# Statistics ahead of the previous norm, a third chunk finished before the last sum, and low halves on VectorE, at the ends of twelve stages

## The reference

```python
def _layernorm(x, axis=-1, eps=1e-05):
    m = jnp.mean(x, axis=axis, keepdims=True)
    v = jnp.var(x, axis=axis, keepdims=True)
    return (x - m) / jnp.sqrt(v + eps)
...
    x = x + 0.5 * _L2_ffn_ref(_layernorm(x, axis=-1), L2_ffn_Wr, L2_ffn_br, L2_ffn_W_up, L2_ffn_b_up, L2_ffn_W_down, L2_ffn_b_down)
    x = x + _L2_attn_ref(_layernorm(x, axis=-1), L2_attn_Wq, L2_attn_bq, L2_attn_Wk, L2_attn_bk, L2_attn_Wv, L2_attn_bv, L2_attn_Wo, L2_attn_bo)
    x = x + 0.5 * _L2_ffn_ref(_layernorm(x, axis=-1), L2_ffn_Wr, L2_ffn_br, L2_ffn_W_up, L2_ffn_b_up, L2_ffn_W_down, L2_ffn_b_down)
```

## Time and profile before

| | us |
|---|---|
| runs of the kernel before | 1792.59, 1788.51, 1789.74 |
| their median | 1789.74 |
| the profiled execution's own time | 1807.28 |
| its span, first to last instruction | 1805.5 |
| TensorE busy in the span | 1522.0 |
| VectorE busy | 1221.4 |
| ScalarE busy | 1022.6 |
| GpSimd busy | 625.2 |

### The profile page before, as it was taken

The page is one execution under the profiler, slowest core; times in us unless marked ns, Lnnn a source line. Parts: engine busy times, 40 slices in busy tenths (PEclk is TensorE's granted clock), DMA queues, the critical chain, the costliest instruction groups (busy, mean ns, idle before and its releaser), DMA issues. The chain is left out here.

```text
span 1805.5 us, 25127 instructions
## 1 busy us (share of the span) xinstructions
PE 1522.0 (84%) x8766; PEld 1050.0 (58%) x8766; DVE 1221.4 (68%) x2789; ACT 1022.6 (57%) x1826; POOL 625.2 (35%) x764
## 2 busy tenths in 40 slices
PE   4998699997899699849989966996696789996696
PEld 3776333333577588538869955995595322223596
DVE  5787688992788743473335956595686688883685
ACT  2653488885554455345537732773374388885274
POOL 3575311122487100123026724673424211111333
PEclk9999899998899799869989978997798899998698
DMA  3121534300220400010000000000564633300574
GB/s 112 46 74 31 118 42 53 53 1 3 84 75 30 158 1 1 0 47 1 1 1 12 1 1 1 2 1 1 154 193 124 158 62 53 53 1 1 135 204 149
DMA packets 100757, 101.05 MB, mean 56 GB/s; under 512 B 23344, under 2 KB 86360, under 8 KB 99769
## 3 DMA queue, kind: packets, MB, share of 16 engines
q1 hardware_dynamic: 97687, 93.39, 21.4%
q0 software_dynamic: 2944, 6.05, 0.9%
HBM read 87.60 MB, written 15.78 MB: 57 GB/s over the span
## 5 line engine op out<-in xcount | busy, mean ns | idle before, releaser
L2617 DVE TENSOR_REDUCE mx<-bank 128x1 f32<-128x512 f32 (+1 forms) x512 | 320.1, 680 | 56.6 <-PE bank L2408 55.8
L2554 ACT ACTIVATE e<-bank 128x512 f32<-128x512 f32 x512 | 273.1, 600 | 50.4 <-PE bank L2440 47.6
L2440 PE MATMUL bank<-qq,kk 99*128 99x512 bf16 (+1 forms) x512 | 164.2, 386 | 12.9 <-ACT e L2554 12.3
L1546 POOL TENSOR_TENSOR midl<-mid,midh 128x512 fp32r<-128x512 f32 (+1 forms) x96 | 126.1, 1320 | 78.4 <-ACT midh L1466 78.3
L2440 PEld LDWEIGHTS bank<-qq,kk 99*128 99x128 bf16 (+1 forms) x512 | 38.8, 97 | 161.9 <-ACT e L2554 123.1
L1051 DVE TENSOR_TENSOR hl<-q,hh 128x512 fp32r<-128x512 f32 x64 | 44.8, 701 | 125.6 <-ACT hh L1021 103.6
L95 PE MATMUL bank<-wdh,midh 128*128 128x256 f32 (+1 forms) x384 | 113.6, 296 | 9.7 <-DVE x L1530 9.7
L226 POOL TENSOR_SCALAR rs<-mv 128x4 f32<-128x4 f32 x48 | 11.4, 237 | 307.5 <-DVE mv L213 306.6
L97 PE MATMUL bank<-wdh,midl 128*128 128x256 f32 (+1 forms) x384 | 111.1, 289 | 0.0
L96 PE MATMUL bank<-wdl,midh 128*128 128x256 f32 (+1 forms) x384 | 110.9, 289 | 0.0
L2047 POOL DMA_INDIRECT token_y<-y,g x60 | 61.2, 1020 | 134.6 <-DVE y L2016 121.5
(11 more groups left out here) (406 smaller groups left out, 4514.0 us busy)
## 6 DMA issues: line engine op xcount, KB each, us to landing
w<-in_L_ffn_W SPq DMA_DIRECT2D x30, 512.0 KB
w<-in_L_ffn_W SPq DMA_DIRECT2D x30, 256.0 KB
qq<-scratch SPq DMA_DIRECT2D x18, 384.0 KB
w<-in_L_ffn_w_kernel SPq DMA_DIRECT2D x16, 344.0 KB
w<-in_L_ffn_w_kernel SPq DMA_DIRECT2D x16, 320.0 KB
wo<-in_L_ffn_wo_kernel SPq DMA_DIRECT2D x16, 320.0 KB
scratch<-e SPq DMA_DIRECT2D x34, 128.0 KB, 5.0
sorted<-in_unsorted SPq DMA_DIRECT2D x2, 1935.0 KB, 10.9
```

The lines of the kernel that those rows point to most:

```text
L1546: e.tensor_tensor(l[0:fn, o], mid[i % 2][0:fn, o], h[0:fn, o].bitcast(F32), ALU.subtract).then_inc(*l2_m_lo.tick(n, i, f))
L2440: e.matmul(b_bank(t, u, j), keys(kk[0:K], t, b)[:, k * 128:(k + 1) * 128], queries(qq[0:K], t, b), start=True, stop=True).then_inc(*at_b.t ...
L2554: e.activation(er[u][:, j * 512:(j + 1) * 512], b_bank(t, u, j), ACT.Exp, bias=0.0, scale=scale).then_inc(*at_e.tick(n, t, u, j))
L2617: e.tensor_reduce(mxa[t % 3][:, o:o + nkb], bank[place_a["a", t, u, j]].rearrange("p (k n) -> p k n", k=nkb), X, ALU.max).then_inc(*at_max ...
```

## The change

Five edits, all at the stage ends:

- `finish_dve` takes the statistics of chunk c ahead of the norm of chunk c - 1, and for c = 3 also ahead of `pre.dve`.
- Stages 1, 3, 5 and 10 are marked `settled`. There VectorE does the norm of chunk 2 before the stage's last sum (`settle_dve`), and the transposes, copy and high half of chunk 2 follow those of chunk 1 at once. In the attention these now stand ahead of the last heads' turn and output product on TensorE and ScalarE.
- The low halves move from GpSimd to VectorE (`halve_dve`), those of layer 1's weights also. In settled stages the first stands ahead of the last sum, two between the statistics and the norm of chunk 3, and one behind that. At m = 9 (stage 8) two stand between statistics and norm, and two behind it. At m = 0 and m = 8 all four stand behind the norm.
- ScalarE writes the high half ahead of the features' copy where it is taken from `xn` (layers 0 and 3), and the copy of `lg` comes last.
- At m = 10 TensorE's closing matmuls stand between the transposes of chunks 1 and 2, not behind those of chunk 3.

SyncE's queue is unchanged, and so are the numbers of operations in all but the engine that does the low halves.

```diff
@@ finish_pe, finish_act: a settled stage also does chunk 2 at its last sum @@
                     features_pe(q, m, c - 2, stage)
+                    if c == 3 and stage.settled:
+                        features_pe(q, m, 2, stage)
...
                     features_act(q, m, c - 2, stage)
                     pre.halve_act(q, c - 2)
+                    if c == 3 and stage.settled:
+                        features_act(q, m, 2, stage)
+                        pre.halve_act(q, 2)
+
+        def settle_dve(q, m, pre):
+
             if m < LAST:
+                norm_dve(q, m, 2)
+                pre.halve_dve(q, 0)
+
+        def finish_dve(q, m, c, pre, ready=None, settled=False):
+            if m < LAST:
+                q.wait_ge(*(ready or xsum.at(m, c)))
+                stats_dve(q, m, c)
                 if c == 3:
                     pre.dve(q)
-                if c > 0:
+                    if settled:
+                        pre.halve_dve(q, 1)
+                        pre.halve_dve(q, 2)
+                    elif scalar_norm(m, 2):
+                        pre.halve_dve(q, 0)
+                        pre.halve_dve(q, 1)
+                if c > 0 and not (c == 3 and settled):
                     norm_dve(q, m, c - 1)
-                q.wait_ge(*(ready or xsum.at(m, c)))
-                stats_dve(q, m, c)
...
@@ begin_pe @@
             for c in range(CHUNKS):
-                if c >= 2:
+                if c == 2:
+                    pre.closing_pe(q)
+                if c == 3 or c == 2 and not stage.settled:
                     features_pe(q, m, c, stage)
...
-            pre.closing_pe(q)
 
         def begin_act(q, m, stage, pre):
             norm_act(q, m, 3)
...
-            for c in (2, 3):
+            pre.closing_act(q)
+            for c in ((3,) if stage.settled else (2, 3)):
+                if pre.from_norm:
+                    pre.halve_act(q, c)
                 features_act(q, m, c, stage)
-            pre.halve_act(q, 2)
+                if not pre.from_norm:
+                    pre.halve_act(q, c)
             if pre.route is not None:
                 q.wait_ge(*route_mm.at(m))
                 q.e.copy(lg_sb[:, :], bank[stage.banks["logits"]][:, 0:128]).then_inc(*logits.tick(m))
-            pre.halve_act(q, 3)
-            pre.closing_act(q)
-
-        def begin_dve(q, m, pre):
+
+        def begin_dve(q, m, stage, pre):
             norm_dve(q, m, 3)
+            for c in range(3 if stage.settled else 2 if scalar_norm(m, 2) else 0, CHUNKS):
+                pre.halve_dve(q, c)
             pre.closing_dve(q)
-
-        def begin_pool(q, m, pre):
-            for c in (2, 3):
-                pre.halve_pool(q, c)
...
@@ layer 1's weights @@
-            def pool(q):
-                low(q, "w1", w_lo)
-                low(q, "w2", w_lo)
+            def closing_dve(q):
+                low(q, "w1", w_set)
+                low(q, "w2", w_set)
...
@@ attention, PE and ACT @@
+                finish_pe(q, m, 3, stage, nxt)
                 if kind == 0:
                     turn(3, bank[0])
                 put_out(3, bank[1], otr[1])
-                finish_pe(q, m, 3, stage, nxt)
...
+                finish_act(q, m, 3, stage, nxt)
                 if kind == 0:
                     turn(3, bank[0])
-                finish_act(q, m, 3, stage, nxt)
...
@@ attention, DVE @@
                     elif s == "o" and u == 3:
+                        if i == 15:
+                            settle_dve(q, m, nxt)
                         close(i)
```

More of the change, by code:

```diff
@@ L68, with __init__ @@
 class Stage:
-    def __init__(self, pe, act, dve, pool, sp, banks=None, free=None):
+    def __init__(self, pe, act, dve, pool, sp, banks=None, free=None, settled=False):
         self.pe, self.act, self.dve, self.pool, self.sp = pe, act, dve, pool, sp
-        self.banks, self.free = banks, free
+        self.banks, self.free, self.settled = banks, free, settled
 class Pre:
-    def __init__(self, sp, buf, pe=None, act=None, dve=None, pool=None, late=None, issue=None, route=None, early=None, halve_act=None, halve_pool=None, loaded=None,
+    def __init__(self, sp, buf, pe=None, act=None, dve=None, pool=None, late=None, issue=None, route=None, early=None, halve_act=None, halve_dve=None, from_norm=False, loaded=None,
                  closing_pe=None, closing_act=None, closing_dve=None):
@@ L83, in __init__ @@
         self.sp, self.buf, self.route, self.loaded = sp, buf, route, loaded
-        self.early, self.halve_act, self.halve_pool = (f or none for f in (early, halve_act, halve_pool))
+        self.from_norm = from_norm
+        self.early, self.halve_act, self.halve_dve = (f or none for f in (early, halve_act, halve_dve))
         self.pe, self.act, self.dve, self.pool, self.late, self.issue = (f or nothing for f in (pe, act, dve, pool, late, issue))
@@ L1070, in down @@
                 def down(c):
+                    if c == 3:
+                        settle_dve(q, m, nxt)
                     for j in range(4):
@@ L1111, in free @@
                     q.wait_ge(*xt_set.at(m, what - 2))
-            stage = Stage(pe, act, dve, pool, sp, {0: 6, 1: 7, 2: 6, 3: 7, "logits": 0}, free)
+            stage = Stage(pe, act, dve, pool, sp, {0: 6, 1: 7, 2: 6, 3: 7, "logits": 0}, free, settled=True)
             return stage, nxt
@@ L2662, in dve @@
                 add(3, bank[1])
-                finish_dve(q, m, 3, nxt)
+                finish_dve(q, m, 3, nxt, settled=True)
             def pool(q):
@@ L2807, in attention @@
             banks = {0: 7, 1: 2, 2: 7, 3: 2, "logits": 3}
-            stage = Stage(pe, act, dve, pool, sp, banks, free)
+            stage = Stage(pe, act, dve, pool, sp, banks, free, settled=True)
             return stage, nxt
@@ L2861, in dve_program @@
                 finish_dve(q, 0, c, first_pre, ready=x_in[c].at())
-            begin_dve(q, 0, first_pre)
+            begin_dve(q, 0, start, first_pre)
             barrier(q, 0)
@@ L2866, in dve_program @@
                 if n + 1 < LAST:
-                    begin_dve(q, n + 1, nxt)
+                    begin_dve(q, n + 1, s, nxt)
                     barrier(q, n + 1)
@@ L2872, in pool_program @@
                 finish_pool(q, 0, c, first_pre)
-            begin_pool(q, 0, first_pre)
             barrier(q, 0)
```

24 lines of the change are left out of this document (10 added, 14 removed).

## The result

| | before | with the change |
|---|---|---|
| median of the runs, us | 1791.16 (4 runs, 1788.51 to 1792.87) | 1763.95 (4 runs, 1762.92 to 1765.77) |
| ratio, 95% interval | | 0.9844, 0.9828 to 0.9860 |
| span of the profiled execution | 1805.5 | 1761.0 |
| granted clock, mean | 0.920 | 0.931 |

The kernel is 27.2 us faster, 1.5%. Two more comparisons, on chips where the kernel before took 1792.3 and 1808.9, gave 0.9839 (0.9815 to 0.9864) and 0.9841 (0.9816 to 0.9865). Forecast were 1765.8 and 24 us.

The account below looks back on a forecast made before the run. Inside stages TensorE was taken as nearest the bound, at the twelve ends unhidden chains before the barrier. Terms summed to 23.9 us, taken as 24 off 1789.7: 1765.8 us, likely 1761 to 1771, range 1754 to 1778 with rivals.

Parts of the forecast that it names:

- the likeliest case: Whole kernel: the shortened end chains come off the span in full, about 1761 to 1771 us; chance 0.59.
- Statistics: End of stage 1: chunk 3's statistics start right after the last sum, not behind chunk 2's norm; 0.93 us less.
- The stalled norm: End of stage 1: chunk 3's norm, no longer beside a GpSimd low half, takes 1.11 instead of 2.05; 0.94 less.
- The tail: End of stage 1: only the barrier is left behind the copy of `lg`; 1.95 less about 0.15, 1.8 us less.
- The blocked `rs`: End of stage 1: two low halves on VectorE hold back GpSimd's addition and power; 0.9 us more, between nothing and 1.4.
- ScalarE's order in the attention: Stage 1: ScalarE does chunk 1 and 2's copies and high halves before the last heads' copy; 0.1 more, at most 1.2.
- Opening: Opening: TensorE's pitch of 3.65 us a chunk decides instead of VectorE's 4.8; 5.1 of 30.83 us less.
- Stage 9: End of stage 9: taking the closing matmuls' results apart lies beside chunks 2 and 3's transposes; 1.2 less, 0.3 to 2.0.
- Stage 0: End of stage 0: norm's chain over 1 us shorter, but query and key pieces stored 1.25 later; 0.7 less, 0 to 1.5.
- A: Stage ends: shorter idle pieces let transposes and router run at 2.4 GHz; 12 us more gain, 1754; chance 0.17.
- B: Next stages' starts, waiting for transfers or the cold clock, give half the gain back; 12 us, 1777.8; chance 0.17.
- C: Stage openings stay longer at 1.2 GHz, making the kernel slower than before; 11 us slower, 1801; chance 0.04.

Follow-up runs that it names:

- second pair: The kernel before and the changed kernel, each unchanged and profiled a second time; 1790.45 us and 1762.51 us.
- first pair: First profiles of the kernel before and of the changed kernel; profiled spans 1805.5 and 1761.0 us.
- third of the change: Third profile of the changed kernel, unchanged, on another chip; 1779.26 us beside 1808.85 for the kernel before.
- five parts undone one at a time: The changed kernel with, in turn: norm ahead of statistics, 0.9881; no stage settled, 0.9865; ScalarE's old order, 0.9901; closing matmuls last, 0.9863; low halves on GpSimd, 1769.29 us.

## Why the prediction was right

The number held (1765.8 against 1764.0, the range 1754 to 1778), and so did the likeliest case: one chain at each end, nothing beside it, and each us taken off it a us off the kernel. The sum of the ends fell by 29.7 us (28.9 for the second pair) and the runs by 27.2, 29.8 and 29.6. So the forecast of 24 was about 5 us too small: 1.5 at stage 9, 0.8 at the opening, 0.5 at stage 0 and small amounts elsewhere in the first pair, where another 1.5 at stage 3 are chance. Step by step:

- **Statistics, 0.93 an end**: 0.04 behind the sum at every end. Right. Undone where the stage isn't settled, it costs 3.0, since at stage 7 TensorE hides it. What settling gives (5.3, or 3.65 net of the blocked `rs`) the prediction had not priced apart.
- **The stalled norm, 0.94**: 1.11 or 1.12 at every end. Right.
- **The tail, 1.95 less 0.15 for the drain**: 0.09 remain, 1.86 less. Right, 0.06 too careful, at six ends.
- **The blocked `rs`, 0.9**: 0.63, 0.34 in the addition and 0.29 in the power. The mechanism was right, its size 0.27 too large: the power began when 0.43 us were left of the second low half, and came out 0.29 longer. At stage 5 only the addition is longer, 0.57.
- **ScalarE's order in the attention, 0.1 to 1.2**: 0.25. In stage 1 the last heads' copy starts 0.97 us behind TensorE's transposes of their output instead of 0.72. The faster output product ahead of the last sum, 0.9 us in stage 1 (0.65 against the second profile), more than pays for it; the prediction didn't have it.
- **Opening, 24.9 to 25.15 for 25.7**: pitch right (TensorE's 3.5 a chunk). From the first statistics to the barrier it is 17.90 us in all three profiles of the change and 23.14 and 23.17 before, 5.25 less for 5.1. The rest is the landing of the input (first statistics at 7.66 and 7.15 before, 6.96 to 7.25 with the change).
- **Stage 9, 1.2 with ends of 0.3 and 2.0**: 2.7, 1.7 and 2.4, above the upper bound in two of three profiles. This term was the worst sized. The bound counted the idle time behind the last closing matmul (1.45) and the copy, and not that the transposes of chunks 2 and 3, now behind the closing matmuls, go wholly or in part at the upper clock: eight of them took 1.04 to 1.60 us in all nine profiles with the move and 1.94 in all five without.
- **Stage 0, 0.7, between 0 and 1.5**: the end is 1.2 shorter, but the first score matmul comes 0.9 us later behind the barrier. From the last sum it is at 13.50 instead of 13.79. The round trip did take over in this profile, as the lower bound had it:

```profile
194.47 0.59 PE L2427 MATMUL bank<-qq,kk 72*128 72x512 bf16 x2 [1.51 <-DMA qq<-scratch]
```

  In the earlier trace rows the same matmul waited for ScalarE; now it waits for the transfer. In the two other profiles of the change it is 13.1 and 13.0 (and in the third the wait is for ScalarE again), in the second of before 15.3. So the gain lies between 0.3 and 2.3 us, and these profiles can't size the term better.
- **Stage 3, 0**: 9.7 to 8.2 in the first pair, but 8.2 in the second profile of before and 9.7 in the third of the change. The change does nothing there.

Of the rivals, A (upper clock at the ends) came true in small part: at stage 9, and in the output product ahead of the last sums of stages 1 and 10, which together is 2 to 2.7 us of its 12. Behind the last sum the four last transposes take 1.09 to 1.12 at the opening and the ends of stages 1, 2, 5, 7, 8 and 10, as before. The prediction had also misread the rows on which A rests. Between its transposes of 0.64 and of 1.11 us TensorE wasn't nearly idle: it did eight router matmuls (441.23, 1.33 us) and then stood still for 1.38 us. With the change it stands still for 2.33 us ahead of the last transposes, so that piece became longer and not shorter. B (half absorbed) has its one place, stage 0, with 0.9 us. C (longer time at 1.2 GHz) is seen in one profile, but no run shows the change as its cause. In a window of 30 us, from 20 us behind the barrier into stage 1, the granted clock was 0.89 before and 0.77 in the first profile of the change, and 0.94 in its second:

```profile
216.22:246.22 30.00, 27.64 (x158) 8.99 (x156) 25.19 (x42) 21.66 (x40) 3.02 (x11) 0.89 0.71 105
```

```profile
208.16:238.16 30.00, 27.64 (x143) 9.23 (x144) 22.13 (x37) 18.75 (x34) 2.62 (x10) 0.77 0.79 130
```

```profile
210.34:240.34 30.00, 26.50 (x160) 8.80 (x161) 25.14 (x42) 21.80 (x40) 3.03 (x11) 0.94 0.79 129
```

In the first profile of the change stage 1 was 3 us longer. Over all profiles its body was 241.9 to 247.8 us, with no order between kernels.

Two of the prediction's own signs came out otherwise. It called a mean clock that moves by over 0.01 a sign of being wrong: in the first pair it moved by 0.011 (0.920 to 0.931), in the second by 0.006 (0.926 to 0.932), and the end of stage 1 and the others became shorter in both alike. And VectorE's idle time ahead of stage 2's first operation is 2.74 us and not about 4, because a low half lies in that piece; from the end of the norm to that operation it is 4.1.

## What to carry to other kernels

Where a barrier closes a stage, write down the chain behind the last sum and look for what stands on it without feeding it: here a norm ahead of statistics, a cast behind a copy, a subtraction on another engine. Price an edit with the others in place, as parts interact: five parts undone one at a time cost 3.0, 3.65, 7.7, 2.3 to 3.4 and 4.5 to 5.2 us, 21 to 23 of 29, and the ScalarE order alone gave 5.4 on the kernel before and 7.7 in the finished one. Compare spans of two profiles only by stage, and take a second profile of the kernel before where a stage that the change doesn't touch moves.

## What was not expected of the hardware

- Stages 9 and 11 take 127.8 to 130.4 us in five profiles and 136 to 139 in the nine others, with nearly equal busy times of all engines. Profiles taken together on one chip share it, and it moves the whole kernel by 16 us, more than half of what the change does. The ratios are the same in both (0.9839 and 0.9841).
- One low half on GpSimd beside a norm on VectorE makes the norm take 2.05 instead of 1.11 us, two 3.01. It is one of the norm's four tile operations that waits: at the end of stage 1 before, the first takes 1.28 us instead of 0.34 and ends at 443.11, 0.08 behind the low half, and the other three take 0.33 each.
- A power on four numbers a partition took 1.33 instead of 1.04 us on GpSimd, where the last 0.43 us of VectorE's second low half lay beside it, and an addition 0.57 instead of 0.23.
- Eight matmuls of the output product took 2.05 to 2.08 us at a granted clock of 0.50 and 1.16 at 1.00.
